# Causal attention in a four-layer block: score columns cut at 64 tokens, sums in a new order, and some masks moved to VectorE

## The chip, the cores and the metric

The kernel runs on one NeuronCore of a Trainium2 chip. The metric is the device time of one launch in microseconds (us), the median of a few runs. The engines are named TensorE (PE in the profile, its weight loads PEld), ScalarE (ACT), VectorE (DVE), GpSimd (POOL) and SyncE (SP, which here issues DMAs). Each engine works through its own instructions in order, and they wait for each other on semaphores.

## What is computed

The input is 16 sequences of 256 tokens of 128 numbers. Four layers follow each other, each added to the stream behind a layer norm: a long convolution, a mixture of eight experts, attention, and the experts again. The attention is where the change lies:

```python
qkv = x @ W_attn.T                       # 4 query sets, one k, one v; 16 heads of 8
for g in range(4):
    q = parts[g].reshape(B, T, 16, 8).transpose(0, 2, 1, 3)
    att = einsum('bhqd,bhkd->bhqk', q, k) * (1 / sqrt(8))
    att = softmax(where(causal, att, -inf))
    outs.append(einsum('bhqk,bhkd->bhqd', att, v))
out = concatenate(outs, -1) @ W_proj.T
```

So each head of each sequence has 4 x 256 queries against 256 keys, and a query sees only keys at or before its own place. In the kernel the second half of each sequence is stored backwards.

## The kernel before

The attention stage works on one sequence (a batch) at a time, and in it on four quads of four heads (lanes). The scores of a quad are made in four steps, so a batch has 16 steps and the stage 256. Scores stand with keys on the partitions and queries (four sets side by side) on the columns.

A step (`tensor_scores`) is three score matmuls of 512 columns, one from each of three lanes; a lane is 32 rows of TensorE. Into one half of a double buffer of three PSUM banks each (`TILE` = 1536 columns) go, by `STEPS_Q`, blocks of first keys (for which a lane needs 2 x 512 columns: four sets, both halves of the queries) and blocks of second keys (512 columns: four sets, the second half of the queries). ScalarE takes the exp of all 1536 columns at once (`scalar_exp`) into one of seven SBUF tiles (`prob`, `PROBS`). A score step may start when the exp two steps back has read its half of the buffer. GpSimd zeroes what lies beyond the diagonal with affine selects on blocks of 128 keys by 128 queries (`gpsimd_mask`, one or two instructions a step). Then TensorE sums v by these weights (`tensor_weigh`, four sums a quad: two of 512 columns, two of 256; the four lanes fill four 32-column parts of the array and add into bank 7). The sums have a column of ones in v, so the softmax denominator comes with them. They run one quad late: those of a quad are made in steps 1, 2 (two of them) and 3 of the next quad, the first of them after VectorE has read bank 7 (semaphore `turned`).

VectorE then transposes bank 7 (`vector_turn`), takes the reciprocal of the denominators and normalises. Beside that, by step number within a batch (`tensor_beside`, `vector_beside`), the other work of the batch is dealt out: step 0 transposes and splits the x of the batch after next (`tensor_at_x`, `vector_at_x_high`, `vector_at_x_low`), step 1 takes statistics for a norm, steps 4, 8 and 12 make and split q and k (`tensor_qk`, `vector_qk_high`, `vector_qk_low`), step 5 turns the output rows (`vector_rows`), steps 7 and 11 project them (`tensor_project`; VectorE adds them in `vector_attended` at its steps 6 and 10), steps 9 and 13 normalise two tiles, step 15 makes v of the next batch (`tensor_v`), which VectorE copies into place at its step 14 (`vector_v`). At steps 2 and 6 VectorE checks the denominators of an earlier batch against bounds (`vector_bounds`). q and k travel through DRAM into stacks of 32 rows a lane (`sync_stack`).

The order on TensorE in a step is: scores, what stands beside, then the sum. The order on VectorE:

```python
for n in range(LAST):
    if n % 4 == 3 and n >= 4:
        vector_turn(e, n // 4 - 1)
    vector_beside(e, *STARTS[n])
```

The functions that the change touches, and what calls them:

Of the kernel before, what the change touches and what calls it, by code (L numbers as in the profile page):

```python
# [17 lines left out]
P = 128  # L18
# [29 lines left out]
PAIRS = SETS // 2  # L48
# [4 lines left out]
BOTH = None  # L53
STEPS_Q = (((0, 0, 0), (1, 0, 0), (2, 1, BOTH)),
           ((2, 0, 0), (3, 0, 0), (0, 1, BOTH)),
           ((1, 1, BOTH), (3, 1, BOTH), (0, 0, 1)),
           ((1, 0, 1), (2, 0, 1), (3, 0, 1)))

SUMS_Q = ((0, 0, 1), (1, 0, 2), (1, 1, 2), (0, 1, 3))
STEPS_B = 4 * QUADS  # L60
PROBS = 7
# [74 lines left out]
def build_in(nc, dr, out, ctx):  # L136
# [28 lines left out]
    in_bounds = sb("in_bounds", [P, P])  # L165
# [47 lines left out]
    with ExitStack() as own:  # L213
# [5 lines left out]
        vstack = sb("vstack", [P, 2, HALVES, 2 * HD + HEADS * SLOT], of=own)  # L219
# [67 lines left out]
    def new_norm(tag):  # L287
# [42 lines left out]
    scored, exped, masked, weighed = (sem(n) for n in (  # L330
        "scored", "exped", "masked", "weighed"))
# [771 lines left out]
    def tensor_at_x(e, b):  # L1103
        e.wait_ge(mixed_norm.out, HALVES * b // FFN_TILES + 1)
        if b == 0:
            e.wait_ge(based, FFN_CHUNKS - 1)
        elif b == 2:

            e.wait_ge(accum, EXPERTS * FFN_CHUNKS - 1)
        else:  # L1110
            e.wait_ge(v_copied, max(1, b - 1))
        for h in range(HALVES):
            last = e.transpose(bank(at_bank(b))[:, h * P:(h + 1) * P], normed[:, HALVES * b + h, :], eye[:])
        last.then_inc(at_up, 1)


    def scalar_at_x_high(e, b):
        e.wait_ge(at_up, b + 1)
        e.copy(at_x[:, b % 2, 0, :], bank(at_bank(b))[:, 0:SEQ]).then_inc(at_high, 1)

    def vector_at_x_high(e, b):
        e.wait_ge(at_up, b + 1)
        e.wait_ge(v_up, b - 1)
        e.tensor_copy(at_x[:, b % 2, 0, :], bank(at_bank(b))[:, 0:SEQ]).then_inc(at_high, 1)

    def vector_at_x_low(e, b):
        e.wait_ge(at_high, b + 1)
        e.tensor_tensor(at_x[:, b % 2, 1, :], bank(at_bank(b))[:, 0:SEQ], at_x[:, b % 2, 0, :], ALU.subtract)\
# [79 lines left out]
    def tensor_v(e, b):  # L1208
# [7 lines left out]
        for h in range(HALVES):  # L1216
            for i, (w_part, x_part) in enumerate(PRODUCTS):
                last = e.matmul(bank(6)[:, h * P:(h + 1) * P], at_x[:, s, x_part, h * P:(h + 1) * P],
                                wqkv_parts[:, w_part, SETS + 1, :], start=(i == 0), stop=(i == len(PRODUCTS) - 1))
        last.then_inc(v_up, 1)  # L1220

    def v_places(b):
        return vstack[:, b % 2, :, 2 * HD:].rearrange("p h (n r) -> p h n r", r=SLOT)[:, :, :, 0:HD]

    def v_source():
        return bank(6)[:, 0:HALVES * D].rearrange("p (h n d) -> p h n d", n=HEADS, d=HD)

    def scalar_v_first(e):
        e.wait_ge(v_up, 1)
        e.wait_ge(zeroed, 3)  # L1230
        e.mul(v_places(0), v_source(), 1.0 / WSCALE).then_inc(v_copied, 1)

    def vector_v(e, b):
        e.wait_ge(v_up, b + 1)
        if b >= 2:
            e.wait_ge(weighed, STEPS_B * (b - 1))
        e.tensor_scalar(v_places(b), v_source(), 1.0 / WSCALE, None, ALU.mult).then_inc(v_copied, 1)
# [6 lines left out]
    def tensor_scores(e, n):  # L1244
# [12 lines left out]
        for i, (lane, keys, pair) in enumerate(STEPS_Q[t]):  # L1257
            at = slice(SLOT * lane, SLOT * (lane + 1))
            if keys == 0:
                queries = qstack[at, s, c, 2 * pair:2 * pair + 2, :].rearrange("p g (h q) -> p h g q", q=P)  # L1260
            else:
                queries = qstack[at, s, c, :, P:SEQ]
            last = e.matmul(to[:, i * BANK:(i + 1) * BANK], kstack[at, s, c, keys * P:(keys + 1) * P], queries, start=True,  # L1263
                            stop=True)
        last.then_inc(scored, 1)

    def scalar_exp(e, n):
        if n >= PROBS:
            q, t = divmod(n - PROBS, 4)
            e.wait_ge(weighed, 4 * q + (3 if t < 2 else 4))  # L1270
        e.wait_ge(scored, n + 1)
        e.activation(prob[:, n % PROBS, :], psum[:, TILE * (n % 2):TILE * (n % 2 + 1)], ACT.Exp, scale=SCALE)\  # L1272
# [4 lines left out]
    def gpsimd_masked(e, kept, second_keys):  # L1277
        sign = -1 if second_keys else 1
        return e.affine_select(kept, kept, [[0, kept.shape[1]], [0, 2], [sign, P]], ALU.is_ge, 0.0, base=0,  # L1279
                               channel_multiplier=-sign)  # L1280

    def gpsimd_mask(e, n):
        t = n % 4
        blocks = prob[:, n % PROBS, :].rearrange("p (n g q) -> p n g q", g=2, q=P)
        e.wait_ge(exped, n + 1)
        if t < 2:
            gpsimd_masked(e, blocks[:, 0:3:2], False)
            gpsimd_masked(e, blocks[:, 4:6], True).then_inc(masked, 1)
        elif t == 2:
            gpsimd_masked(e, blocks[:, 0:4], True)  # L1290
            gpsimd_masked(e, blocks[:, 4:5], False).then_inc(masked, 1)
        else:
            gpsimd_masked(e, blocks[:, 0:5:2], False).then_inc(masked, 1)

    def weights_of(n, lane, keys, pair):

        t, i = next((t, i) for t, banks in enumerate(STEPS_Q) for i, held in enumerate(banks)
                    if held[:2] == (lane, keys) and held[2] in (pair, BOTH))
        ring = prob[:, (n + t) % PROBS, i * BANK:(i + 1) * BANK]
# [885 lines left out]
```

## Time and profile before

| | |
|---|---|
| median of 3 runs | 800.98 us (800.91 to 801.03) |
| the profiled execution | 800.58 us |
| its span, first to last instruction | 798.9 us |
| attention stage (first scores to last exp) | 244.08 to 607.30 us of the span |
| PE / ACT / DVE / POOL busy | 95% / 90% / 81% / 70% of the span |
| mean granted TensorE clock | 0.996 |

Busy shares are means over stages with different limits. TensorE's rows are modelled at their ends: a row of matmuls is longer than the engine is held, so the distance between starts of what follows without a wait says more than a length.

### The profile page before, as it was taken

The numbers are of one execution on the slowest core, as the hardware profiler recorded it, in microseconds if no ns is written. First come the engines' busy times: TensorE is split into PE (matmuls) and PEld (weight loads), VectorE is DVE, ScalarE is ACT, GpSimd is POOL, SyncE is SP. The second block draws the span as 40 slices with busy tenths as digits, with TensorE's granted clock in tenths as the row PEclk, the third lists the DMA queues.
The fourth block names the chain that finished last, engine by engine and source line by source line (L and its number), as shares of the span: only waits on it lengthen the run. The fifth ranks groups of instructions, "written<-read, shape, count | busy, mean of one in ns | idle before, by whom it ended". The sixth has DMA issues, their size and how long they took to land.

```text
span 798.9 us, 20426 instructions
## 1 busy us (share of the span) xinstructions
PE 757.4 (95%) x7674; PEld 412.7 (52%) x7674; DVE 648.9 (81%) x1917; ACT 719.9 (90%) x932; POOL 560.2 (70%) x685
## 2 busy tenths in 40 slices
PE   5898999999999999999999999999999999999996
PEld 3345667777774333333333333333334777677774
DVE  7998999999876667777778787788566898989885
ACT  5918999999999999999999999999997999899984
POOL 2897676655437888888898888888896445444442
PEclk9999999999999999999999999999999999999999
DMA  9110000000133333442444334433500000000000
GB/s 279 61 70 29 1 2 2 2 2 1 23 94 99 98 90 89 90 99 78 96 108 106 90 88 92 90 78 96 106 2 2 1 15 16 15 14 16 15 15 18
DMA packets 37962, 45.70 MB, mean 57 GB/s; under 512 B 6137, under 2 KB 23810, under 8 KB 37858
## 3 DMA queue, kind: packets, MB, share of 16 engines
q1 hardware_dynamic: 37858, 44.33, 22.4%
q8 instruction: 63, 1.03, 0.6%
q14 instruction: 41, 0.34, 0.2%
HBM read 27.53 MB, written 16.78 MB: 55 GB/s over the span
## 4 chain that ended last, share of the span: by engine, by line
PE 56%; ACT 18%; DVE 12%; issue 10%; POOL 2%; DMA 0%; ACTq 0%; DVEq 0%; POOLq 0%
PE psum L1006 15%; PE psum L937 14%; ACT prob L1272 13%; PE psum L1316 12%; PE psum L1263 5%; PE psum L1374 4%; DVE mixed L1025 4%; PE psum L1154 2%; ACT hidden_first L951 2%; ACT hidden_parts_first L953 1%; PE psum L686 1%; DVE hidden_parts_first L960 1%; POOL yhat L666 1%; DVE prod L656 1%; DVE stats L362 1%
## 5 line engine op out<-in xcount | busy, mean ns | idle before, releaser
L1272 ACT ACTIVATE prob<-psum 128x1536 f32<-128x1536 f32 x256 | 347.6, 1503 | 14.5 <-PE psum L1263 14.5
L1279 POOL TENSOR_SCALAR_AFFINE_SELECT prob<-prob 128x512 f32<-128x512 f32 (+3 forms) x448 | 304.8, 709 | 42.2 <-ACT prob L1272 32.1
L1316 PE MATMUL psum<-prob,vstack 128*32 128x256 f32 (+1 forms) x2048 | 204.9, 495 | 1.6 <-DVE o_tok L1324 1.6
L937 PE MATMUL psum<-xt_parts,w_parts 128*128 128x512 f16 x768 | 186.6, 379 | 0.0
L1025 DVE SCALAR_TENSOR_TENSOR mixed<-psum,comb_y,mixed 128x128 f32<-128x128 f32 x512 | 143.1, 339 | 1.5 <-PE psum L1006 1.5
L967 POOL TENSOR_TENSOR hidden_parts_second<-hidden_second,hidden_parts_second 128x512 f16<-128x512 f32 x64 | 77.2, 1207 | 93.6 <-ACT hidden_parts_second L953 93.6
L967 POOL TENSOR_TENSOR hidden_parts_first<-hidden_first,hidden_parts_first 128x512 f16<-128x512 f32 x64 | 79.4, 1241 | 73.2 <-ACT hidden_parts_first L953 73.2
L1263 PE MATMUL psum<-qstack,kstack 32*128 32x512 f16 x768 | 99.8, 385 | 9.1 <-ACT prob L1272 7.7
L1263 PEld LDWEIGHTS psum<-qstack,kstack 32*128 32x128 f16 x768 | 24.9, 91 | 157.3 <-ACT prob L1272 138.7
L937 PEld LDWEIGHTS psum<-xt_parts,w_parts 128*128 128x128 f16 x768 | 71.0, 98 | 64.0 <-issue 1.4
L951 ACT ACTIVATE hidden_second<-psum,b 128x512 f32<-128x512 f32 x128 | 88.3, 690 | 15.6 <-PE psum L937 12.1
L1006 PEld LDWEIGHTS psum<-w_parts,hidden_parts_first 128*128 128x128 f16 x1536 | 90.4, 98 | 19.4 <-issue 6.1
L1006 PE MATMUL psum<-w_parts,hidden_parts_first 128*128 128x128 f16 x1536 | 96.2, 219 | 3.8 <-DVE mixed L1025 3.4
L1006 PEld LDWEIGHTS psum<-w_parts,hidden_parts_second 128*128 128x128 f16 x1536 | 90.9, 98 | 16.2 <-issue 2.1
L1006 PE MATMUL psum<-w_parts,hidden_parts_second 128*128 128x128 f16 x1536 | 96.0, 219 | 1.0 <-POOL hidden_parts_second L967 0.5
L951 ACT ACTIVATE hidden_first<-psum,b 128x512 f32<-128x512 f32 x128 | 90.4, 706 | 7.0 <-PE psum L937 6.2
L953 ACT ACTIVATE hidden_parts_first<-psum,b 128x512 f16<-128x512 f32 x128 | 90.6, 708 | 0.0
L953 ACT ACTIVATE hidden_parts_second<-psum,b 128x512 f16<-128x512 f32 x128 | 88.4, 691 | 0.0
L1324 DVE STREAM_TRANSPOSE o_tok<-psum 128x512 f32<-128x512 f32 x64 | 45.9, 716 | 44.5 <-PE psum L1316 43.6
L1316 PEld LDWEIGHTS psum<-prob,vstack 128*32 128x32 f32 x2048 | 46.8, 108 | 52.8 <-issue 29.4
L960 DVE TENSOR_TENSOR hidden_parts_second<-hidden_second,hidden_parts_second 128x512 f16<-128x512 f32 x64 | 56.2, 878 | 18.9 <-ACT hidden_parts_second L953 18.8
L960 DVE TENSOR_TENSOR hidden_parts_first<-hidden_first,hidden_parts_first 128x512 f16<-128x512 f32 x64 | 48.9, 765 | 14.9 <-ACT hidden_parts_first L953 14.9
(148 smaller groups left out, 840.9 us busy)
## 6 DMA issues: line engine op xcount, KB each, us to landing
qstack<-qk_parts SPq DMA_DIRECT2D x128, 128.0 KB, 3.6
qk_parts<-parts SPq DMA_DIRECT2D x64, 192.0 KB, 3.1
kstack<-qk_parts SPq DMA_DIRECT2D x128, 32.0 KB, 3.5
stream<-u_folded SPq DMA_DIRECT2D x4, 512.0 KB, 8.0
kept_x<-stream SPq DMA_DIRECT2D x4, 512.0 KB, 2.7
out<-mixed SPq DMA_DIRECT2D x7, 256.0 KB, 2.3
w_whole<-L_ffn_W SPq DMA_DIRECT2D x1, 1024.0 KB, 8.9
taps<-c_taps SPq DMA_DIRECT2D x1, 640.0 KB, 7.1
```

Of the source, the lines that this page charges most:

```text
L937: last = e.matmul(bank(u % 4), m.w1[:, w_part, ex, cols], xt_parts[:, s, x_part, :], start=(n == 0), stop=(n == len(PRODUCTS) - 1))
L951: last = e.activation(m.hidden[:, r, k, :], bank(u % 4), ACT.Relu, scale=scale, bias=bias)
L953: last = e.activation(m.hidden_parts[:, r, 0, k, :], bank(u % 4), ACT.Relu, scale=scale, bias=bias)
L960: e.tensor_tensor(m.hidden_parts[:, r, 1, 0, :], m.hidden[:, r, 0, :], m.hidden_parts[:, r, 0, 0, :], ALU.subtract).then_inc(low_first, 1)
L967: e.tensor_tensor(m.hidden_parts[:, r, 1, 1, :], m.hidden[:, r, 1, :], m.hidden_parts[:, r, 0, 1, :], ALU.subtract).then_inc(low_second, 1)
L1006: last = e.matmul(down_place(m, ch, ex, t), h_[:, t * P:(t + 1) * P], w_, start=(n == 0), stop=(n == len(terms) - 1))
L1025: last = e.scalar_tensor_tensor(out=m.y[:, t0 + t, :], in0=down_place(m, ch, ex, t), scalar=comb_y[:, s, t, ex:ex + 1], in1=m.y[:, t0 + t, ...
L1263: last = e.matmul(to[:, i * BANK:(i + 1) * BANK], kstack[at, s, c, keys * P:(keys + 1) * P], queries, start=True, stop=True)
L1272: e.activation(prob[:, n % PROBS, :], psum[:, TILE * (n % 2):TILE * (n % 2 + 1)], ACT.Exp, scale=SCALE)\
L1279: return e.affine_select(kept, kept, [[0, kept.shape[1]], [0, 2], [sign, P]], ALU.is_ge, 0.0, base=0, channel_multiplier=-sign)
L1316: last = e.matmul(to[SLOT * lane:SLOT * (lane + 1)], vstack[:, b % 2, keys, first:first + SLOT], weights_of(n - t, lane, keys, pair), star ...
L1324: e.transpose(o_tok[:, r, :], bank(7)).then_inc(turned, 1)
```

## The change

Everything is now cut at 64 tokens (`BLK`) instead of 128. Of the four blocks of 64 by 64 in each causal triangle one is never seen, and it is no longer computed. For a lane there are three kinds of scores: EARLY (the first 64 keys of each half against all queries of that half, 512 columns), LATE (the other 64 keys of each half against the later 64 queries, 256 columns), and ACROSS (keys of the second half against queries of the first, in stored order, 512 columns, all seen in full, without a mask). A step holds two banks of EARLY or ACROSS and 256 columns of LATE: 1280 columns (`COLS`). Keys of both halves lie on partitions 0 to 63 and 64 to 127, so each block of scores takes two matmuls of 64 output rows, six a step. The sums are three a quad, ACROSS first, then EARLY, then LATE (256 columns), one each in steps 1, 2 and 3 of the next quad. v lies in three arrangements, which takes more and smaller products (`tensor_v`) and three copies (`v_moves`); `tensor_at_x` transposes the second half twice; `vector_rows` takes three transposes; the bounds are checked every four batches on four times the width. The ring has eight exp tiles.

GpSimd masks 768 columns (the EARLY banks and the LATE part) of steps 0 and 1 twice each, one pass for each half, and the LATE parts of steps 2 and 3 together (512 columns) twice, in quads 0 and 2 of a batch. In quads 1 and 3 VectorE masks those 512 columns by one multiply with a table `seen` of zeros and ones, built once.

```diff
-SUMS_Q = ((0, 0, 1), (1, 0, 2), (1, 1, 2), (0, 1, 3))
+STEPS_Q = (((EARLY, 0, 0), (EARLY, 1, BANK), (LATE, 2, 2 * BANK)),
+           ((EARLY, 2, 0), (EARLY, 3, BANK), (LATE, 1, 2 * BANK)),
+           ((ACROSS, 0, 0), (ACROSS, 1, BANK), (LATE, 3, 2 * BANK)),
+           ((ACROSS, 2, 0), (ACROSS, 3, BANK), (LATE, 0, 2 * BANK)))
+COLS = 2 * BANK + SETS * BLK
+SUMS_Q = (ACROSS, EARLY, LATE)
+VECTOR_LATE = (1, 3)
+PROBS = 8
+BOUNDED = 4
 tensor_at_x:
-        for h in range(HALVES):
+        for at, h in ((0, 1), (P, 1), (P + BLK, 0)):
 tensor_v:
-        for h in range(HALVES):
+        for kind in (EARLY, LATE, ACROSS):
             for i, (w_part, x_part) in enumerate(PRODUCTS):
+                for half in range(HALVES if kind != ACROSS else 1):
+                    rows = slice(BLK * half, BLK * (half + 1)) if kind != ACROSS else slice(0, P)
+    def v_moves(b):
+        for half in range(HALVES):
+            rows = slice(BLK * half, BLK * (half + 1))
+            yield places[rows, 0:2, :, half], source[rows, 0:2]
+        yield places[:, ACROSS, :, 0], source[:, ACROSS]
 tensor_scores:
+            for half in range(HALVES):
+                rows = slice(BLK * half, BLK * (half + 1))
+                if kind == EARLY:
+                    key, moving, place = P * half, queries[:, half], to[rows, col:col + BANK]
+                elif kind == LATE:
+                    key, moving, place = P * half + BLK, queries[:, half, 1], to[rows, col:col + SETS * BLK]
+                else:
+                    key, moving, place = P + BLK * half, queries[:, 0], to[rows, col:col + BANK]
+                last = e.matmul(place, kstack[at, s, c, key:key + BLK], moving, start=True, stop=True)
+    def vector_late(e, q):
+        e.wait_ge(exped, 4 * (q + 1))
+        if q == VECTOR_LATE[0]:
+            e.wait_ge(seen_set, 3)
+        kept = late_place(q)
+        e.tensor_tensor(kept, kept, seen[:].rearrange("p (n g q) -> p n g q", n=1, g=1).to_broadcast([P, 2, SETS, BLK]),
+                        ALU.mult).then_inc(late_multiplied, 1)
+    def gpsimd_mask(e, n):
+        q, t = divmod(n, 4)
+        if t == 0:
+            gpsimd_early_second_half(e, q, 0)
+            if q and (q - 1) % QUADS not in VECTOR_LATE:
+                gpsimd_late_first_half(e, q - 1)
+        elif t == 1:
+            gpsimd_early_second_half(e, q, 1)
+            gpsimd_early_first_half(e, q, 0)
+            gpsimd_early_first_half(e, q, 1)
+        elif t == 3 and q % QUADS not in VECTOR_LATE:
+            gpsimd_late_second_half(e, q)
 tensor_weigh, before a LATE sum:
+            e.wait_ge(late_multiplied if c in VECTOR_LATE else late_masked, late_count(q))
 vector_rows:
-        e.transpose(o_rows[:].rearrange("p a h k t -> p (a h k t)"), o_norm[:].rearrange("p a n r -> p (a n r)"))\
+        for late in range(2):
+            e.transpose(rows[:, :, 1 - late], blocks[:, :, late])
+        e.transpose(o_rows[:, 1].rearrange("p g t -> p (g t)"), o_norm[:, 1].rearrange("p n r -> p (n r)"))\
 vector_attention:
             vector_beside(e, *STARTS[n])
+            if n % 4 == 1 and n >= 4 and (n // 4 - 1) % QUADS in VECTOR_LATE:
+                vector_late(e, n // 4 - 1)
```

## Rows read from the trace of the kernel before

**Rows 1.** Stages: batches 0, 7, 14, 15; columns: stretch, length, busy us (instructions).

```profile
core 0: us, PE busy (x) PEld busy (x) DVE busy (x) ACT busy (x) POOL busy (x), PEclk, DMA share, GB/s
244.08:266.16 22.08, 20.27 (x218) 8.19 (x217) 15.04 (x41) 21.38 (x17) 19.46 (x28) 1.00 0.30 75
402.06:424.70 22.64, 22.34 (x219) 8.18 (x215) 17.36 (x39) 21.71 (x17) 20.07 (x30) 1.00 0.44 95
...
561.14:583.33 22.19, 20.23 (x202) 6.75 (x198) 10.65 (x22) 21.64 (x17) 19.10 (x29) 1.00 0.42 87
583.33:607.30 23.97, 20.92 (x212) 7.26 (x212) 18.17 (x59) 23.53 (x20) 22.30 (x32) 1.00 0.01 2
```

**Rows 2.** ScalarE: timeline (start, length, instructions) and a group (busy, mean ns).

```profile
397.40 16.23 ACT L1272 ACTIVATE prob<-psum 128x1536 f32<-128x1536 f32 x12 [0.66 <-PE psum L1263]
413.90 1.45 ACT L1272 ACTIVATE prob<-psum 128x1536 f32<-128x1536 f32 x1 [0.28 <-PE psum L1263]
L951 ACT ACTIVATE hidden_second<-psum,b 128x512 f32<-128x512 f32 x128 | 88.3, 690 | 15.6 <-PE psum L937 12.1
```

**Rows 3.** TensorE: timeline of one inner batch.

```profile
400.63 0.51 PE L1218 MATMUL psum<-wqkv_parts,at_x 128*128 128x128 f16 x6
401.06 1.07 PE L1316 MATMUL psum<-prob,vstack 128*32 128x512 f32 x8
402.06 0.39 PE L1263 MATMUL psum<-qstack,kstack 32*128 32x512 f16 x3
402.39 0.44 PE L1113 MATMUL psum<-eye,normed 128*128 128x128 f32 x2
402.93 0.39 PE L1263 MATMUL psum<-qstack,kstack 32*128 32x512 f16 x3
403.25 1.07 PE L1316 MATMUL psum<-prob,vstack 128*32 128x512 f32 x8
...
404.60 1.07 PE L1316 MATMUL psum<-prob,vstack 128*32 128x256 f32 x16
...
405.94 1.07 PE L1316 MATMUL psum<-prob,vstack 128*32 128x512 f32 x8
406.96 0.39 PE L1263 MATMUL psum<-qstack,kstack 32*128 32x512 f16 x3
407.29 0.83 PE L1154 MATMUL psum<-at_x,wqkv_parts 128*128 128x256 f16 x6
...
411.32 1.16 PE L1374 MATMUL psum<-wproj,o_rows 128*128 128x128 f32 x8
...
413.40 0.39 PE L1263 MATMUL psum<-qstack,kstack 32*128 32x512 f16 x3
...
419.54 0.39 PE L1263 MATMUL psum<-qstack,kstack 32*128 32x512 f16 x3
```

**Rows 4.** Waits in 402.06 to 424.70: us in total, times, longest.

```profile
PEld psum L1263 <- ACT prob L1272: 8.4, 13, 0.9
```

**Rows 5.** VectorE: timeline in the same batch.

```profile
401.17 0.42 DVE L1237 TENSOR_SCALAR vstack<-psum 128x256 f32<-128x256 f32 x1 [0.70 <-PE psum L1218]
402.20 0.72 DVE L1324 STREAM_TRANSPOSE o_tok<-psum 128x512 f32<-128x512 f32 x1 [0.60 <-PE psum L1316]
...
403.34 0.82 DVE L1329 TENSOR_TENSOR o_norm<-o_tok,rden 128x256 f32<-128x256 f32 x1
...
406.25 0.74 DVE L1352 SCALAR_TENSOR_TENSOR in_bounds<-rden,in_bounds 128x128 f32<-128x128 f32 x1
407.07 0.72 DVE L1324 STREAM_TRANSPOSE o_tok<-psum 128x512 f32<-128x512 f32 x1
...
408.21 0.49 DVE L1329 TENSOR_TENSOR o_norm<-o_tok,rden 128x256 f32<-128x256 f32 x1
...
409.34 0.69 DVE L1184 SCALAR_TENSOR_TENSOR parts<-psum,parts 128x512 f16<-128x512 f32 x1
409.95 1.23 DVE L1339 STREAM_TRANSPOSE o_rows<-o_norm 128x1024 f32<-128x1024 f32 x1
```

**Rows 6.** GpSimd: mask groups by shape, 300 to 590 us (busy, mean ns).

```profile
L1279 POOL TENSOR_SCALAR_AFFINE_SELECT prob<-prob 128x512 f32<-128x512 f32 x204 | 126.1, 643 | 31.2 <-ACT prob L1272 26.6
L1279 POOL TENSOR_SCALAR_AFFINE_SELECT prob<-prob 128x768 f32<-128x768 f32 x51 | 44.5, 872 | 0.0
```

**Rows 7.** GpSimd and VectorE at 586.79: a bounds instruction behind the end of two masks.

```profile
585.61 1.23 POOL L1279 TENSOR_SCALAR_AFFINE_SELECT prob<-prob 128x512 f32<-128x512 f32 x2 [0.40 <-ACT prob L1272]
586.79 0.28 DVE L1352 SCALAR_TENSOR_TENSOR in_bounds<-rden,in_bounds 128x128 f32<-128x128 f32 x1
```

**Rows 8.** VectorE: the normalising group in 402.07 to 424.70 (busy, mean ns).

```profile
L382 DVE TENSOR_SCALAR normed<-stream,meanvar,rstd 128x128 f32<-128x128 f32 x4 | 1.5, 428 | 0.0
```

**Rows 9.** GpSimd: the clearing in the first expert stage.

```profile
137.95 1.86 POOL L1637 MEMSET vstack<- 128x2112 f32 x1
```

More of the change, by code:

```diff
@@ L1256, in tensor_scores @@
             e.wait_ge(s_stack[s], STACK * (b // 2 + 1))
-        for i, (lane, keys, pair) in enumerate(STEPS_Q[t]):
+        for kind, lane, col in STEPS_Q[t]:
             at = slice(SLOT * lane, SLOT * (lane + 1))
[L1259 to L1264, printed above, removed]
+            queries = qstack[at, s, c].rearrange("p g (h l q) -> p h l g q", h=HALVES, q=BLK)
+            for half in range(HALVES):
[7 more added lines that the diff above has]
+                last = e.matmul(place, kstack[at, s, c, key:key + BLK], moving, start=True, stop=True)
         last.then_inc(scored, 1)
@@ L1295, in weights_of, with gpsimd_masked @@
[L1295 to L1299, printed above, removed]
-        return ring if keys == 0 else ring[:, pair * SEQ:(pair + 1) * SEQ]
-    def tensor_weigh(e, n):
-        b, c, t = step_of(n)
-        keys, pair, needs = SUMS_Q[t]
-        if n % STEPS_B == 0:
-            e.wait_ge(v_copied, b + 1)
-        if n == 0:
-            e.wait_ge(accum, EXPERTS * FFN_CHUNKS)
-        elif t == 0:
-            e.wait_ge(turned, n // 4)
-        e.wait_ge(masked, n - t + needs + 1)
-        to = bank(7) if keys == 0 else bank(7)[:, SEQ:2 * SEQ]
+    def gpsimd_masked(e, kept, half):
+        sign = 1 if half else -1
+        return e.affine_select(kept, kept, [[0, n] for n in kept.shape[1:-1]] + [[sign, BLK]], ALU.is_ge, 0.0,
+                               base=BLK * half, channel_multiplier=-sign)
@@ new lines, in gpsimd_mask, with weights_of @@
+    def gpsimd_mask(e, n):
+        q, t = divmod(n, 4)
[9 more added lines that the diff above has]
+            gpsimd_late_second_half(e, q)
+    def weights_of(q, kind, lane):
+        t, col = next((t, at) for t, held in enumerate(STEPS_Q) for of, head, at in held if (of, head) == (kind, lane))
+        return prob[:, (4 * q + t) % PROBS, col:col + (SETS * BLK if kind == LATE else BANK)]
@@ L1314, in tensor_weigh @@
         for lane in range(LANES):
[L1315 to L1317 removed]
+            last = e.matmul(to[SLOT * lane:SLOT * (lane + 1)],
+                            vstack[:, b % 2, kind, c * LANES + lane].rearrange("p h r -> p (h r)"),
+                            weights_of(q, kind, lane), start=(kind == ACROSS), stop=(kind == LATE))
```

180 lines of the change are left out of this document (102 added, 78 removed).

## The prediction

> **What bounds the kernel now.** I read four views: the stages, the waits, one batch of the attention stage instruction by instruction on three engines, and the groups by shape.
>
> The change touches the attention stage, 244.08 to 607.30 us of the span. Its 16 batches take about 22.64 us each, the first 22.08 and the last two 22.19 and 23.97 [rows 1]. In an inner batch ScalarE is busy 21.7 us, TensorE 22.3, VectorE 17.4 and GpSimd 20.1, so no engine has much room. ScalarE's exp of 1536 columns is the pace: twelve in a row fill 16.23 us, that is one alone (1.45) and eleven at 1.344 [rows 2]. Sixteen make 21.5; the missing 1.1 us comes at the two projections, where TensorE is late.
>
> TensorE is hardly slower than that pace. From starts that follow each other [rows 3]: three score matmuls S = 0.33 (402.93 to 403.25), a weighted sum over 512 columns W = 1.00 (405.94 to 406.96 is 1.02), two sums of 256 columns together also 1.0, so one alone about 0.57 (half the 0.86 of streaming, and the 0.14 that any sum has beside it), V = 0.44, transposes A = 0.45, q and k products Q = 0.76 (0.83 less the drain that overlaps) twice and 0.43 for the half-sized third, projection P = 1.09. A batch: 16 S + 12 W + 5.0 (V, A, 2 Q and the third, 2 P) = 22.3 of 22.64. That the score loads wait 8.4 us for ScalarE [rows 4] is mostly loads standing ready early: matmuls behind them still run. So if ScalarE gets faster, TensorE follows at once, and then it matters who else is late.
>
> VectorE is [rows 5]. After the v copy (401.17) and the turn of a quad (402.20) it works without a gap until 407.0, and the next turn (407.07) starts just when its sum is ready (405.94 + 1.02). The rows of the projection end at 411.18 and the projection starts at 411.32. Both times it is just in time.
>
> **The change part by part.** I name quads of a batch c0 to c3 and steps n0 to n15; the three sums of a quad run in the steps 1, 2 and 3 of the next quad (c3's in n1 to n3 of the next batch).
>
> *ScalarE.* 256 columns less an exp. From 512 columns (690 ns) to 1536 (1.45 us alone) the slope is 0.74 ns a column; the mean of the pace is 0.875 [rows 2]. I take 0.21 us: pace 1.13, 18.1 a batch. That alone would be 256 x 0.21 = 54 us, if nothing else bound.
>
> *TensorE.* Sums: across 512, early 512, late 256: 2.57 for 3.0 a quad, 1.7 less a batch. Scores: the same 32-row lanes, each as two halves of 64 output rows, six matmuls for three. That column parts of the array run beside each other the sums show (8 matmuls on four 32-column parts in 1.07 us), that row parts do the scores (three in 0.39) [rows 3]; both at once no row shows. Bounds: 0.33 if they overlap, 0.33 + 0.21 if a lane's halves run after each other. The rows show both kinds of overlap, so I take 0.33. V becomes 15 matmuls, 12 of them half wide: between 9 and 15 pitches of 0.055 and a switch (V's 0.44 is six such and 0.11), 0.6 to 1.05 for 0.44; I take 0.75. The transposes A: three for two, 0.60. Sum of a batch: 16 x 0.33 + 4 x 2.57 + (0.60 + 1.95 + 0.75 + 2.18) = 21.0. So TensorE alone would already stop the pace far above ScalarE's 18.1.
>
> *GpSimd.* Four masks of 768 columns a quad (mean 872, pitch 0.82) and, in every second quad, two of 512 (pitch 0.59) [rows 6]: 15.5 a batch for about 19. It has room, but its instructions are longer.
>
> *VectorE.* Added: the late multiply of 512 columns twice a batch. No row has it; the nearest is 0.68 to 0.69 (512 columns, 409.34) [rows 5]. The v copy is three instructions: 0.42 + 0.42 + 0.29 and gaps, 0.97 to 1.3, for 0.42. The rows' transpose is three for one of 1.23: between 0 and 0.4 more, I take 0.25. The bounds go from two a batch (0.74 the one at 406.25) to two, four times as wide, in four batches.
>
> *What a multiply waits for.* An instruction of VectorE with two SBUF tensors stands while GpSimd is in a mask: the bounds of 128 columns took 0.74 at 406.25, with masks running, and 0.28 at 586.79, where the mask had just ended [rows 5, 7]. The normalisation of a quad took 0.82 and 0.49 likewise. A running mask of 768 can therefore cost the multiply 0 to 0.86; I take 0.35. (The Trainium skill, "SBUF — State Buffer", on who interferes with whom: the port pair is held by whichever starts first for its whole instruction, and the other is blocked. The trace agrees, 0.74 against 0.28; without the rule the multiply would be 0.69 flat and the forecast about 6 us lower, 0.35 in 12 first stretches and some 0.1 in 12 fourth ones.)
>
> *The new wait.* The late sum of c3 (step n3) now waits for the multiply, which stands in VectorE's order behind the v copy, the turn of c2, its reciprocal and normalisation, the two x copies and the statistics of step n1. Count from the end of V. VectorE: v starts at 0.11 and ends at 1.31; the turn to where the bounds instruction now starts is 402.20 to 406.25, 4.05, less 0.2 for a mean normalisation: 5.2; lock 0.35, multiply 0.69, signal 0.13 (as from the rows' end 411.18 to 411.32), and 0.1 of gaps: 6.47. TensorE is ready after late c2 0.57, S, A 0.60, and S + W twice, S: 4.5. So it stands about 2 us, with everything behind the sum on its in-order queue: next scores, hence ScalarE.
>
> Against the batch before, stretch by stretch [rows 3, 5]:
> - scores n0 to the end of c3's last sum: 4.90 before (402.06 to 406.96). Now 6.47 + 0.57 less the 0.57 of late c2 at the head = 6.47. **+1.57**
> - from there to the projection: 4.36 before (to 411.32). VectorE now 0.11 + 4.11 (407.07 to 411.18) + 0.25 + 0.13 = 4.60; TensorE alone 4.08. **+0.24**
> - projection and last sum: 2.08 before (to 413.40), now 1.09 + 0.57. **-0.42**
> - n8 to the end of c1's last sum: 6.14 before (413.40 to 419.54). Now VectorE: 0.11, turn, reciprocal, normalisation and q/k copies 2.96 (407.07 to 410.03), two tiles normalised 0.43 + 0.43 [rows 8], lock, multiply and signal 1.17, in all 5.1, against TensorE's 5.2 (4 S, Q, 2 W, P); then 0.57: 5.8. **-0.35**
> - n12 to n0: 5.16 before (to 424.70), now 4 S + 0.43 + 2 W + 0.75 + 0.57 = 5.07. **-0.09**
>
> Sum +0.95 for an inner batch. Of these there are 11 (2 to 11 and 13): +10.5. Batch 12, whose range checks already slow it, +0.6. Batch 1 has no statistics in n1 (1.5 less in the chain): -0.5. Batch 0 has neither chain nor projection: near ScalarE's pace, 19.5 for 22.08: -2.6. Batch 14 has no q and k work: about 20.3 for 22.19, -1.9. Batch 15 likewise, with its waits for v: 21.1 for 23.97, -2.9. GpSimd's clearing of v places grows from 2112 to 3072 columns (1.86 us, so 0.9 more [rows 9]) and the table's selects; in the expert stage GpSimd idles over a microsecond an expert, I charge 0.5. Together +3.7. The expert stages are as before. The profiled execution took 800.58 (span 798.9 and 1.7 around it), 0.4 under the median of 800.98; so 804.7 for the median.
>
> **The rivals.**
> 1. *The chain on VectorE is short* (multiply not blocked, normalisation 0.42, v 0.97, rows no longer): the first stretch +0.79, then 0, -0.42, -0.49, -0.25 = -0.37 a batch; with the edge batches' -7.4 that is 12 x -0.37 - 7.4 = -11.8, so 789, and up to 799 where only some of these hold. For it: the phases of masks and VectorE shift, and 0.42 occurs. Against: GpSimd still masks 15.5 of 23 us, three masks in a row just at step n1. It decides where the multiply is done within 5.5 us of V's end.
> 2. *TensorE alone bounds*: 21.0 a batch, 12 x -1.6 and the edges -8: about 773. It needs VectorE's chain under 4.5 us, and even the shortest count gives 5.7.
> 3. *ScalarE goes on setting the pace*: 801 - 54 = 747. TensorE's sum speaks against it.
> 4. *A lane's halves do not overlap*: +0.21 a step. Where VectorE sets the stretch it hides, elsewhere it shows. By stretch: 6.47 unchanged, 4.9 and 6.0 plus 0.57 where TensorE now leads, 5.9 for 5.07, so about 2 us a batch on my case and some 3 in each edge batch: 804.7 + 12 x 2 + 4 x 3 = 841. For it: no row has both partings at once. (The Trainium skill, "TensorEngine Tiling (Array Packing)", tiling modes, lists 32x64 as eight independent tiles, and under restrictions that column tiling gives up the fast weight load; the trace has no score load of 64 columns, and the first would keep 0.33, the second puts it towards this rival.)
>
> **How the numbers follow.** My case 0.55, and as it reaches from 799 to 822 with the bounds of lock and v, I put 0.15 of it within 0.2% (1.6 us, about what a measurement of this kernel can tell from no change) and 0.40 above. Rival 1 0.22, rival 2 0.10, rival 3 0.03, rival 4 0.10. So faster 0.35, same 0.15, slower 0.50. The range runs from rival 1's low end, 789, to my case with its unknown terms at their upper ends: the lock 0.86 for 0.35 at both multiplies, the normalisation at its full 0.82, the rows 0.4 longer for 0.25, 1.4 a batch in 12 batches, 17 us, so 822. With 0.77 for these two cases and a little of the others that fall inside, it holds about 0.8.
>
> **What would show it.** Exps at a pace of 1.13 where they follow each other; an inner batch of 23.6 us; score groups still 0.33 to the next start; in step n3 a TensorE wait of about 2 us for the multiply, the largest new row of the waits; multiplies of 0.69 and of over 1 us; GpSimd down to some 70% of a batch. If the wait in n3 is under 1 us or score groups take 0.5, the prediction is wrong there.

## The result and the profile after

The changed kernel takes 823.46 us (822.05 to 825.52, four executions) against 800.94 for the kernel before: ratio 1.0285, interval 1.026 to 1.031. It is slower by 22.5 us, and outside my range, which ended at 822. In the profiled executions (the one after was the longest of its four) the span went from 798.9 to 823.8, so 24.9 us more: 1.5 ahead of the attention stage (first scores at 245.59 instead of 244.08), 23.0 in it, 0.4 behind it.

The windows of an inner batch and, below it, of a stretch in batch 0 that is taken up again under the clock; they answer to [rows 1] and have its columns:

```profile
core 0: us, PE busy (x) PEld busy (x) DVE busy (x) ACT busy (x) POOL busy (x), PEclk, DMA share, GB/s
389.49:413.78 24.29, 21.25 (x245) 7.77 (x242) 20.58 (x44) 19.32 (x17) 18.64 (x23) 1.00 0.40 88
264.00:268.30 4.30, 4.30 (x35) 0.71 (x34) 3.38 (x7) 3.32 (x3) 3.28 (x5) 0.60 0.20 43
```

An inner batch takes 24.29 us (22.64 before). ScalarE is down to 19.3 of it and GpSimd to 18.6, as meant; VectorE is up from 17.4 to 20.6. What TensorE waits for is in the waits of the stretch 365.70 to 389.50, in which L1348 is the multiply, L1387 the sums, L1296 the scores, L1417 the rows and L1454 the projection (this batch is one of the two with the wide bounds instruction, 0.42 us longer than the others):

```profile
ACT prob L1303 <- PE psum L1296: 4.8, 4, 1.7
PEld psum L1387 <- DVE prob L1348: 2.6, 2, 1.5
PE psum L1387 <- DVE prob L1348: 2.1, 2, 1.2
...
PEld psum L1454 <- DVE o_rows L1417: 1.2, 1, 1.2
PE psum L1454 <- DVE o_rows L1417: 0.9, 1, 0.9
```

The late sums stand twice a batch for the multiply, 2.1 us, and ScalarE stands for the scores behind them. The places are in TensorE's timeline:

```profile
365.63 0.52 PE L1127 MATMUL psum<-eye,normed 128*128 128x128 f32 x3 [0.44 <-DVE vstack L1264]
...
367.75 1.07 PE L1387 MATMUL psum<-prob,vstack 128*32 128x512 f32 x8
368.75 0.41 PE L1296 MATMUL psum<-qstack,kstack 32*64 32x512 f16 x6
370.35 0.64 PE L1387 MATMUL psum<-prob,vstack 128*32 128x256 f32 x8 [1.19 <-DVE prob L1348]
...
381.77 1.16 PE L1454 MATMUL psum<-wproj,o_rows 128*128 128x128 f32 x8
383.85 0.64 PE L1387 MATMUL psum<-prob,vstack 128*32 128x256 f32 x8 [0.92 <-DVE prob L1348]
...
388.19 0.80 PE L1238 MATMUL psum<-wqkv_parts,at_x 128*64 128x128 f16 x15
388.92 0.64 PE L1387 MATMUL psum<-prob,vstack 128*32 128x256 f32 x8
389.49 0.41 PE L1296 MATMUL psum<-qstack,kstack 32*64 32x512 f16 x6
```

The first wait for the multiply (step n3, quad c3) I had forecast, the second (step n11, quad c1) not, nor the 0.44 us that the transposes A (L1127) wait for the three v copies. VectorE's timeline shows what stood in front of each multiply:

```profile
366.87 0.41 DVE L1141 CAST at_x<-psum 128x256 f16<-128x256 f32 x1
367.32 0.42 DVE L1145 TENSOR_TENSOR at_x<-psum,at_x 128x256 f16<-128x256 f32 x1
367.66 0.86 DVE L374 BATCH_NORM_STATS2 stats<-stream 128x6 f32<-128x128 f32 x4
368.56 0.38 DVE L378 BATCH_NORM_AGGREGATE meanvar<-stats 128x2 f32<-128x6 f32 x4
368.97 0.74 DVE L384 TENSOR_SCALAR vareps<-meanvar 128x4 f32<-128x4 f32 x1
369.61 0.68 DVE L1348 TENSOR_TENSOR prob<-prob,seen 128x512 f32<-128x512 f32 x1
...
380.00 0.69 DVE L1201 SCALAR_TENSOR_TENSOR parts<-psum,parts 128x512 f16<-128x512 f32 x1
380.60 1.87 DVE L394 TENSOR_SCALAR normed<-stream,meanvar,rstd 128x128 f32<-128x128 f32 x2
382.39 1.40 DVE L1348 TENSOR_TENSOR prob<-prob,seen 128x512 f32<-128x512 f32 x1
```

GpSimd's timeline beside them:

```profile
367.92 3.14 POOL L1312 TENSOR_SCALAR_AFFINE_SELECT prob<-prob 128x768 f32<-128x768 f32 x3 [0.20 <-ACT prob L1303]
...
380.63 3.68 POOL L1312 TENSOR_SCALAR_AFFINE_SELECT prob<-prob 128x768 f32<-128x768 f32 x4 [0.22 <-ACT prob L1303]
```

In the first place an instruction over four columns (L384) takes 0.74 us, and the multiply behind it 0.68. In the second the two normalisings take 1.87 together, where one alone had a mean of 0.43 [rows 8], and the multiply takes 1.40. Both lie inside a run of masks. I call such an instruction held: its row is longer than that of the same instruction elsewhere. It goes both ways: the last of the three masks from 367.92 begins at 369.64, just behind the start of the free multiply, and lasts 1.42 us where the two before it last 0.91.

I cut each batch by the starts of scores n0, n4, of the projection, of n8, n12 and the next n0, as in the prediction:

| inner batch | n0-n4 | -projection | -n8 | n8-n12 | n12-n0 | sum |
|---|---|---|---|---|---|---|
| before | 4.90 | 4.36 | 2.08 | 6.14 | 5.16 | 22.64 |
| forecast | 6.47 | 4.60 | 1.66 | 5.79 | 5.07 | 23.6 |
| measured | 6.13 | 4.66 | 1.66 | 6.75 | 5.08 | 24.29 |

(24.71 in the two inner batches with the wide bounds instruction, 1.38 us.) Batch 0 takes 24.25, batch 13 27.4, batches 14 and 15 20.42 and 25.34.

### The profile page after: what moved, and what is told of

Same layout as the page of the kernel before. It is cut to its first block, busy times and chain, and to the rows that moved or that the text cites. A ratio compares the mean times of both kernels' runs of the same rounds, so it can differ in the third digit from the quotient of the medians.

```text
span 823.8 us, 21206 instructions
## 1 busy us (share of the span) xinstructions
PE 746.6 (91%) x8090; PEld 407.9 (50%) x8090; DVE 702.7 (85%) x1987; ACT 681.1 (83%) x934; POOL 539.0 (65%) x562
## 4 chain that ended last, share of the span: by engine, by line
PE 49%; DVE 35%; issue 7%; ACT 5%; POOL 3%; DMA 0%; DVEq 0%; ACTq 0%; POOLq 0%
PE psum L1018 14%; PE psum L949 13%; PE psum L1387 10%; DVE mixed L1037 4%; DVE o_tok L1397 4%; DVE normed L394 3%; DVE prob L1348 3%; PE psum L1454 2%; PE psum L1296 2%; DVE parts L1196 2%; DVE vstack L1264 2%; DVE stats L374 2%; DVE rden L1400 2%; ACT hidden_parts_first L965 2%; ACT hidden_first L963 2%
## 5 line engine op out<-in xcount | busy, mean ns | idle before, releaser
L1303 ACT ACTIVATE prob<-psum 128x1280 f32<-128x1280 f32 x256 | 307.8, 1238 | 76.1 <-PE psum L1296 68.3
L1312 POOL TENSOR_SCALAR_AFFINE_SELECT prob<-prob 128x768 f32<-128x768 f32 (+1 forms) x320 | 282.7, 913 | 85.5 <-ACT prob L1303 84.5
L1387 PE MATMUL psum<-prob,vstack 128*32 128x512 f32 (+1 forms) x1536 | 181.5, 545 | 33.0 <-DVE prob L1348 28.4
L1296 PE MATMUL psum<-qstack,kstack 32*64 32x512 f16 (+1 forms) x1536 | 104.5, 366 | 1.2 <-ACT prob L1303 1.1
L1296 PEld LDWEIGHTS psum<-qstack,kstack 32*64 32x64 f16 x1536 | 30.0, 101 | 149.2 <-ACT prob L1303 117.6
L1387 PEld LDWEIGHTS psum<-prob,vstack 128*32 128x32 f32 x1536 | 30.5, 109 | 74.6 <-DVE prob L1348 35.7
```

The costliest lines, as they stand in the source:

```text
L1296: last = e.matmul(place, kstack[at, s, c, key:key + BLK], moving, start=True, stop=True)
L1303: e.activation(prob[:, n % PROBS, 0:COLS], psum[:, TILE * (n % 2):TILE * (n % 2) + COLS], ACT.Exp, scale=SCALE)\
L1312: return e.affine_select(kept, kept, [[0, n] for n in kept.shape[1:-1]] + [[sign, BLK]], ALU.is_ge, 0.0, base=BLK * half, channel_multipli ...
L1387: last = e.matmul(to[SLOT * lane:SLOT * (lane + 1)], vstack[:, b % 2, kind, c * LANES + lane].rearrange("p h r -> p (h r)"), weights_of(q, ...
```

## The experiments

All edits are on the changed kernel unless said otherwise; ratios are to the kernel before, whose medians lay near 800.9. Stretches are cut as above, in batch 2.

### All masks on GpSimd

```diff
-VECTOR_LATE = (1, 3)
+VECTOR_LATE = ()
 VectorE, in the second expert stage:
-                    vector_late(e, LAST // 4 - 1)
 gpsimd_attention, at its end:
+        gpsimd_late_first_half(e, LAST // 4 - 1)
```

> The changed kernel with GpSimd masking the late keys of every quad, as it does in quads 0 and 2; no multiply on VectorE. In the changed kernel an inner batch takes 24.29 us, in stretches 6.13 (scores n0 to n4), 4.66 (to the projection), 1.66, 6.75 (n8 to n12) and 5.08. Theory A, the late sums of quads 3 and 1 wait for the multiply behind VectorE's other work: the first stretch falls to about 4.9 and the fourth to 5.8, as in batch 1 of the changed kernel (4.87, 5.76), the others stay; a batch of 22.1, the clock no longer falls, and the whole is 788 to 795 us. Theory B, GpSimd is too full (19 us of masks and rstd in a batch of 22, and its masks hold up VectorE's two-input instructions): late sums wait for GpSimd instead, batches of 23 us or more, 805 us or more. Theory C, the loss is in TensorE's smaller products and the v copies: batches stay over 23.5 us and the whole over 815.

Measured: 791.58 us (791.37 to 791.95), ratio 0.9872 [0.9843, 0.9901]; stretches 4.87, 4.35, 1.66, 5.76, 5.08, in all 21.72. Theory A holds: without the multiplies on VectorE the change is no longer slow. With GpSimd doing all the masks the rest of the change gains 0.92 us a batch on the kernel before, and in an inner batch TensorE never waits for GpSimd (in the whole stage twice, 1.7 us together). This version beats both kernels, by 1.3% the one before. The clock did not behave as expected: it still falls once, just behind the stage. An inner batch is 0.7 us above the 21.0 that I had counted for TensorE alone; its two waits for VectorE, 0.44 and 0.18, are most of that:

```profile
PE psum L1127 <- DVE vstack L1264: 0.4, 1, 0.4
PE psum L1454 <- DVE o_rows L1417: 0.2, 1, 0.2
```

### The multiply on 8 of 512 columns

The late keys of quads 1 and 3 stay nearly unmasked here.

```diff
-        kept = late_place(q)
-        e.tensor_tensor(kept, kept, seen[:].rearrange(...).to_broadcast([P, 2, SETS, BLK]),
+        kept = late_place(q)[:, :, :, 0:1]
+        e.tensor_tensor(kept, kept, seen[:, 0:1].rearrange(...).to_broadcast([P, 2, SETS, 1]),
```

> The changed kernel with the multiply cut to one column of each block of 64 (8 columns of 512), in the same place of VectorE's order; the late keys of quads 1 and 3 are left unmasked but for these. Theory A in the form 'its place in the order costs': only the instruction's own 0.5 to 0.6 us goes each time, stretches 5.6 and 6.2, batch 23.2, whole about 805. In the form 'the instruction itself, with its wait for masks, costs': also the blocked time of the second one (1.40 against 0.68) goes, stretches 5.6 and 5.8 or less, batch 22.8, whole about 798. Theory C: 818 or more.

Measured: 809.8 us (808.25 to 811.06), ratio 1.0096 [1.0063, 1.013]; 5.62, 4.67, 1.66, 6.24, 5.08, in all 23.25. Its VectorE timeline:

```profile
293.81 0.74 DVE L384 TENSOR_SCALAR vareps<-meanvar 128x4 f32<-128x4 f32 x1
294.45 0.16 DVE L1348 TENSOR_TENSOR prob<-prob,seen 128x8 f32<-128x8 f32 x1
```

The arithmetic of the multiplies, 0.52 each, is worth 1.04 of the 2.57 us a batch (24.29 less the 21.72 with none); the place in VectorE's order and what is held there are worth the rest. That is the first form of the expectation; the whole is 5 us above it, and part of that is a clock fall in batch 13. In batches 2 to 11 the small multiplies take 0.16 or 0.88 (five of the 32, outside these batches, 0.50 to 0.87): the 0.72 of being held is the same for 8 columns as for 512.

### The multiply ahead of the work beside

```diff
+            if n % 4 == 0 and n >= 4 and (n // 4 - 1) % QUADS in VECTOR_LATE:
+                vector_late(e, n // 4 - 1)
             vector_beside(e, *STARTS[n])
-            if n % 4 == 1 and n >= 4 and (n // 4 - 1) % QUADS in VECTOR_LATE:
-                vector_late(e, n // 4 - 1)
```

> The changed kernel with the multiply at the head of VectorE's work of the step before (step 0 and 8 instead of the end of step 1 and 9), so ahead of the x copies and statistics, and ahead of the q and k copies and the norm. Theory A: nothing waits for it any more, stretches one and four fall to 4.9 and 5.8, but the work behind it is later by 0.7 to 1.4 us: q and k of step 8 and the projections may wait; batch 22.1 to 22.6, whole 788 to 800. Theory B, the multiply is blocked by masks wherever it stands and delays the rest of VectorE as much: the waits move to the projection and to bank 6, batch 23.5 or more, whole over 812. Theory C: over 818.

Measured: 805.25 us (803.0 to 806.51), ratio 1.0045 [1.003, 1.006]; 4.87, 5.21, 1.66, 5.76, 5.08, in all 22.59. The waits of the late sums are gone, so both stalls are a matter of the queue. But the work did not vanish. Against the first experiment's kernel the stretch to the projection is 5.21 instead of 4.35, since the rows (L1417) now come late (TensorE waits 0.66 us for them); c3's multiply is itself held, 1.38 us, where it now stands. Of the 2.57 us a batch a third is given back there, more in the two batches with the wide bounds (23.5), and the whole came out 5 us above theory A's range.

### The clearing split

```diff
-        e.memset(vstack[:], 0.0).then_inc(zeroed, 1)
+    def gpsimd_clear_first(e, s):
+        e.memset(vstack[:, s], 0.0).then_inc(zeroed, 1)
...
+                if (ch, ex) in ((3, 1), (3, 3)):
+                    gpsimd_clear_first(e, ex // 2)
```

with the table built two experts later.

> The changed kernel with GpSimd's clearing of the v places, ones, bounds and table spread over four experts of the first expert stage instead of one. In the changed kernel the first scores start 1.5 us later than before (245.59 against 244.08) and the hidden blocks fall behind between 142 and 155 us. If the longer clearing is the cause, the first scores come at 244 to 244.3 and the whole is 1.3 us shorter (0.15%, hardly more than the spread); if it is not, they stay at 245.6.

Measured: 821.92 us (821.63 to 825.28), ratio 1.0263 [1.0225, 1.0301]. First scores at 245.21, of 245.59: between my two outcomes. The hidden blocks near 150 us are 0.5 behind the kernel before instead of 1.4, but the expert stage loses another 0.7 at 222 us, in this kernel and the changed one alike. The inner batches are unchanged at 24.28. Its profile serves for the clock, below.

### The q and k copies on ScalarE

```diff
-            vector_qk_high(e, b + 2, at // 4 - 1)
 scalar_attention, behind scalar_exp(e, n):
+            if b + 2 < BATCH and at in (4, 8, 12):
+                if at == 4:
+                    e.wait_ge(s_parts[b % 2], 64 * ((b + 2) // 2))
+                scalar_qk_high(e, b + 2, at // 4 - 1)
```

> The changed kernel with the three copies of q and k of steps 4, 8 and 12 (0.68 us each on VectorE) given to ScalarE, which idles 5 us of a batch there. Stretches of the changed kernel: 6.13, 4.66, 1.66, 6.75, 5.08. Theory A, a chain in VectorE's order: the first stretch has no such copy in its chain and stays 6.13, the second falls by up to 0.6 to TensorE's own 4.1, the fourth by about 0.7 to 6.0 or 6.1, or by more where the multiply then falls between masks; batch 22.9 to 23.1, whole 800 to 808. Rival, VectorE is simply too full (its share of busy time counts, not what stands ahead of the sum): every stretch shortens, the first too. Rival, ScalarE's exps come late behind the copies: no gain, 820 or more.

Measured: 804.88 us (803.68 to 806.07), ratio 1.0044 [1.0031, 1.0057]; 6.13, 4.31, 1.66, 5.76, 5.08, in all 22.95, as expected. With 0.68 us less in front of it the multiply of c1 is also free, at 0.68, so the whole 0.99 of the fourth stretch goes. The first, where no copy was moved, keeps its 6.13.

### Masks of one column in 64

GpSimd leaves nearly all masking out, VectorE's multiply is whole.

```diff
+        few = 1 if len(kept.shape) > 3 else BLK
+        if few == 1:
+            kept = kept[:, :, :, 0:1]
-        return e.affine_select(kept, kept, [...] + [[sign, BLK]],
+        return e.affine_select(kept, kept, [...] + [[sign, few]],
```

> The changed kernel with GpSimd's masks cut to one column in 64, so that GpSimd hardly reads SBUF beside VectorE; nearly all masking of quads' early keys and of quads 0 and 2 is left out, the table and VectorE's multiplies stay whole. Theory B, masks hold up VectorE's instructions: all multiplies take 0.68 instead of 0.68 and 1.40, the normalising of two tiles ahead of the second takes 0.7 us instead of 1.9; stretch four falls from 6.75 to 5.76, TensorE's own; stretch one has no held-up multiply and stays within 0.1 of 6.13; batch 23.2, whole about 805. If the masks don't hold VectorE up, nothing changes: 24.3 and 823.

Measured: 792.48 us (792.18 to 793.1), ratio 0.9893 [0.9874, 0.9912]; 5.58, 4.36, 1.66, 5.76, 5.08, in all 22.43. VectorE's groups in 291.9 to 316.2 (busy, mean ns), first of the changed kernel:

```profile
L394 DVE TENSOR_SCALAR normed<-mixed,meanvar,rstd 128x128 f32<-128x128 f32 x4 | 3.2, 850 | 0.0
L1348 DVE TENSOR_TENSOR prob<-prob,seen 128x512 f32<-128x512 f32 x2 | 2.1, 1040 | 0.0
L384 DVE TENSOR_SCALAR vareps<-meanvar 128x4 f32<-128x4 f32 x1 | 0.7, 740 | 0.0
```

and of this kernel, where L1351 is the multiply:

```profile
L1351 DVE TENSOR_TENSOR prob<-prob,seen 128x512 f32<-128x512 f32 x3 | 2.1, 685 | 0.0
L394 DVE TENSOR_SCALAR normed<-mixed,meanvar,rstd 128x128 f32<-128x128 f32 x4 | 1.2, 373 | 0.0
L384 DVE TENSOR_SCALAR vareps<-meanvar 128x4 f32<-128x4 f32 x1 | 0.2, 170 | 0.0
```

Same instructions, same shapes; only GpSimd's masks are short. All 32 multiplies take 0.68 to 0.69 here. So the masks hold them, not only the multiply but also the norm's instructions, which read and write one tensor each in SBUF (and read per-partition scalars beside it). Being held is worth 24.29 - 22.43 = 1.86 us a batch. The whole kernel is 31 us faster, but that is not all holding: this kernel has no clock fall either, and the falls of the changed kernel took about 6 us of its profiled execution (below). I had expected only the fourth stretch to fall; the first fell too, by 0.55, the length by which L384 had been held.

### The exp back to 1536 columns, all masks on GpSimd

On the first experiment's kernel; the 256 columns more are values that nothing reads.

```diff
-prob[:, n % PROBS, 0:COLS], psum[:, TILE * (n % 2):TILE * (n % 2) + COLS]
+prob[:, n % PROBS, 0:TILE], psum[:, TILE * (n % 2):TILE * (n % 2) + TILE]
```

> The kernel with all late keys masked by GpSimd (791.6 us, batch 21.72), but each exp over 1536 columns as before the change; the last 256 columns are left over values that nothing reads. It tells what the narrower exp is worth. By my count of TensorE (21.0 to 21.7 a batch with ScalarE at 18.1) the fewer columns are worth only what lies between TensorE's 21.7 and ScalarE's old pace with its stalls, 22.6: batch 22.5 to 22.7, edges 1 us each, whole 803 to 807. Rival, the whole gain comes from TensorE's smaller sums and the exp is worth nothing: 792 to 794. Rival, ScalarE set the pace all along: 0.21 x 256, 840 or more.

Measured: 796.11 us (793.43 to 797.84), ratio 0.9934 [0.9912, 0.9956]; 5.02, 4.37, 1.66, 5.76, 5.08, in all 21.89. My count missed, the rival came near: the shorter exp is worth 0.17 us an inner batch of the 0.92. The medians differ by 4.5 us, but of that the clock has a part: in the profiled execution it is at half for 6.9 us in batch 15, which takes 26.27 instead of 22.52. The rest of the inner batch's gain is TensorE's, above all the third and fourth stretches (1.66 for 2.08, 5.76 for 6.14) with their smaller sums.

### All masks on GpSimd, copies on ScalarE, clearing split

The edits of the first, fourth and fifth experiments together.

> Late keys of all quads on GpSimd, q and k copies on ScalarE, the clearing spread over four experts. From 791.6 us: the second stretch 4.35 falls to TensorE's own 4.1 (-3 us in 12 batches, and some in batches 12 and 13), the first scores come 0.4 to 1.4 us earlier; 785 to 788. Rival, ScalarE (18.1 and 1.5 us of a batch of 21.5) now comes late with its exps at the copies: 792 or more.

Measured: 791.55 us (790.82 to 792.25), ratio 0.9881 [0.9861, 0.9901]; 4.87, 4.53, 1.66, 5.76, 5.08, in all 21.90. The rival's mechanism was right, at the edge of its 792: the copy now queues behind an exp on ScalarE, VectorE waits 0.82 us for it and the rows come later, so TensorE waits 0.35 us for them instead of 0.18. There was little to win on VectorE by then.

### One multiply at a time

```diff
-VECTOR_LATE = (1, 3)
+VECTOR_LATE = (3,)
```

> The changed kernel with VectorE masking the late keys of quad 3 alone, GpSimd those of quad 1 too. If the two waits add up stretch by stretch: 6.13 for the first stretch as with both, 5.76 for the fourth as with none, batch 23.3, whole 806 to 810. If they interact (GpSimd's fuller row of masks shifts what VectorE is held up by), the first stretch moves by more than 0.3 from 6.13.

Measured: 808.31 us (807.31 to 810.0), ratio 1.0093 [1.0059, 1.0126]; 6.13, 4.67, 1.66, 5.76, 5.08, in all 23.30. And with `VECTOR_LATE = (1,)`:

> The changed kernel with VectorE masking the late keys of quad 1 alone. Added stretch by stretch: 4.87 for the first as with none, 6.75 for the fourth as with both, batch 22.7 to 23.0, whole 801 to 807. If the fourth stretch falls to 6.1 or less, its extra time came from how the masks fell and not from the multiply's place.

Measured: 806.56 us (804.37 to 808.85), ratio 1.0066 [1.0045, 1.0086]; 4.87, 4.35, 1.66, 6.76, 5.08, in all 22.72. Both as expected (the second has a clock fall in batch 0, the first none), and they add up: c3's multiply costs 1.58 a batch (first and second stretch), c1's 1.00 (fourth), together the 2.57 between 21.72 and 24.29.

### The turn ahead of the v copy

On the first and fourth experiments' edits: the turn of c2 before the v copy, the transposes A in step 3, the x copies in step 2.

```diff
-        if b + 2 < BATCH and at == 0:
-            tensor_at_x(e, b + 2)
+        if b + 2 < BATCH and at == 3:
+            tensor_at_x(e, b + 2)
 and in vector_beside: vector_at_x_high at 2 (of 0), vector_v at 15 (of 14)
```

> All late keys on GpSimd, the clearing spread, and the step before the batch's end reordered: VectorE turns quad 2 before it copies v, TensorE's transposes of x come in step 3 instead of step 0 and VectorE's x copies in step 2. In the kernel with all late keys on GpSimd the transposes of step 0 wait 0.4 us for the three v copies to leave bank 6. If that wait is what the first stretch of 4.87 holds over TensorE's own 4.4, it falls to 4.4 to 4.7, batch 21.3 to 21.5, whole 785 to 790. Rival: the x copies now come late for q and k of step 4, the second stretch grows by as much, whole 791 or more.

Measured: 796.06 us (794.43 to 796.52), ratio 0.9931 [0.9907, 0.9955]; 4.62, 4.55, 1.66, 5.76, 5.08, in all 21.67. The rival was right: the first stretch gave 0.25, as expected, and the second took 0.20 back. Batch 15 lost 2.9 us (25.37 for 22.52): in its step n0 TensorE waits 2.67 us for the v copies, and the clock falls to half for 3.5 us behind it. As a whole this order is worse than the plain one.

## Why the prediction was wrong

The sign was right, and so was the mechanism of the first stretch, a late sum that waits for VectorE's chain and multiply. The size was not: I forecast 3.7 us more, the spans differ by 24.9.

**What held.** Score groups of six matmuls are 0.34 to the next start (366.08 to 366.42), so rival 4 is out: halves of a lane overlap. V takes 0.73 (388.19 to 388.92) for my 0.75. The third stretch is 1.66 and the fifth 5.08, both as counted. The second is 4.66 for 4.60. Batch 1 is 0.6 faster, batch 14 1.8, as forecast (0.5 and 1.9). The wait in step n3 is there, 1.19 us for the 2 I gave. The multiply of c3 was not held (0.68, I had 1.04), but L384 in front of it was (0.74, alone 0.17), and from V's end to the late sum it was 6.14 us (364.21 to 370.35) for my 6.47. TensorE was ready 0.44 later than I counted, because its transposes A wait for the v copies; that shortens the wait, not the stretch, which came out 0.34 shorter than I said. I had put 0.35 of holding on the multiply, and 0.57 fell on L384 instead: that this stretch came out near is partly luck. Rivals 1 to 3 needed a short chain on VectorE; taking the multiply off VectorE altogether gives 791.6, near rival 1's low end, and even then it isn't rival 2's 773. (Rival 1's fourth stretch, 0.49 less, lay below what I had counted for TensorE alone, 5.2 + 0.57; with the multiplies gone it is 0.38 less.)

**The step that failed** is the fourth stretch, "-0.35": it came out +0.61, 0.96 worse in each of ten batches, and batches 0 and 13 have the same 6.75. I had VectorE done with the multiply of c1 after 5.1 us, just ahead of TensorE's 5.2. The late sum started after 6.19 (377.66 to 383.85), so VectorE's chain ended last, by a microsecond. Two terms of it were too small. I charged "two tiles normalised 0.43 + 0.43" from a mean of the kernel before [rows 8]; the pair took 1.79 from its start to the multiply's. And I gave a lock of 0.35; the multiply took 1.40, so 0.72 of holding. I had applied the rule of being held to the instructions with two SBUF tensors alone. The masks-cut kernel shows that the norm's instructions are held too (0.373 for 0.850 us on average), and the mean of rows 8 already hid one: of its four instructions three last 0.34 to 0.38 and one 0.66, the same in every batch from 300 to 425 us. And I had spread the hold as a mean, while each of batches 2 to 11 repeats the last to 0.01 us: there the multiply of c3 is always free and that of c1 always held. What the hold comes to depends on the place: besides 0.72, L384 has 0.57 here, 0.07 in the inner batches of the first experiment's kernel (0.24 us), and four multiplies in batches 12, 14 and 15 have 0.34 to 0.55. I think that a late multiply moves the next exps and their masks with it, so that the same instruction meets the same mask in each batch; no run tests that.

**The edge batches.** Of the miss of 21 us the ten batches 2 to 11 have 7.8, for in them the first stretch pays back a third. Batches 0, 13 and 15 have 12.8 (24.25, 27.4, 25.34 against my 19.5, 23.6, 21.1), the start of the stage 1.0 and the end 0.4; batch 12 is 0.8 better than I said (23.02 for 23.8). For batch 0 I had counted no chain on VectorE, but c1's multiply stands there too: TensorE waits 2.01 us for it. With all masks on GpSimd these three batches take 20.75, 22.50 and 22.52, together 1.6 over my counts, so nearly all of the 12.8 comes with the multiplies. Part of that is the same holding: with the masks cut they take 20.0, 23.1 and 21.3. Part is TensorE's clock. In the profile after, the granted clock is at half (the 1.2 GHz level) at 264.3 to 267.8, 564.7 to 571.5 and 626.2 to 629.6 us; before, it stays whole through the attention stage. At half, eight sums last 1.94 us where they last 1.06:

```profile
262.61 0.64 PE L1387 MATMUL psum<-prob,vstack 128*32 128x256 f32 x8 [2.01 <-DVE prob L1348]
...
263.95 0.41 PE L1296 MATMUL psum<-qstack,kstack 32*64 32x512 f16 x6
264.29 1.94 PE L1387 MATMUL psum<-prob,vstack 128*32 128x512 f32 x8
266.16 0.64 PE L1296 MATMUL psum<-qstack,kstack 32*64 32x512 f16 x6
266.73 1.54 PE L1387 MATMUL psum<-prob,vstack 128*32 128x512 f32 x8
```

The kernel with the split clearing has the same inner batches and no fall inside the stage; its batches 0, 13 and 15 take 22.67, 24.77 and 23.44. The differences, 1.6, 2.6 and 1.9, put the cost of the falls in the profiled execution at 6.1 us, some of which that kernel loses again to a fall just behind the stage (its rest is 2.9 longer). The median is 2 us below the profiled execution, so it may hold less of them.

**The start.** I charged 0.5 for the clearing and the table, and the stage starts 1.5 later. GpSimd's group in the first expert stage lasts 4.55 us instead of 2.2, and the hidden block behind it starts 1.4 later; the idle time there did not cover it, though half a microsecond comes back by 162 us. But the clearing is not all of it, since spreading it gave back only 0.4. At 222 us the changed kernel and the split-clearing one both lose 0.7 (0.3 of it comes back): there ScalarE waits for the fifteen products V of batch 0, 0.5 us with the split clearing, and copies them in three instructions instead of one. I had charged nothing for that.

**What stays open.** Why the clock falls where it does isn't settled: ahead of 264.3 and of 564.7 the split-clearing kernel has the same TensorE stalls of 2 us and does not fall there. That masks hold the norm's instructions is shown by cutting the masks; that they do so through a shared way into SBUF is only argued. (The Trainium skill, "SBUF — State Buffer", on who interferes with whom, puts it down to a shared port pair, and names beside instructions with two SBUF inputs those of VectorE in a two-port mode, which I had passed over. The runs agree in that either engine is held by the other, and in that the holds of the attention stage given here, 0.07 to 0.72, are all shorter than a mask; whether the norm's instructions run in that mode no run shows.) Nor have I traced why batch 13 is slower than the other inner batches even with the masks cut (23.09 for 22.43).

## What to carry to other kernels

Before moving work from an idle-looking engine to another, list what stands in front of it in the new queue, at its held duration: the masks had room on GpSimd (with all of them there the kernel takes 791.6 us, and no other version is clearly faster), and the multiplies cost 2.57 us a batch on VectorE for 1.4 us of work. Where two engines can hold each other, count each instruction at the place that the schedule gives it, as free or as held, up to the length of the other's instruction, and do the forecast for both; where the batches repeat each other, the same case comes in all of them. And put edge batches into the sum with the same care as inner ones: here three of sixteen carried 12.8 of the 21 us.

## What was unexpected of the hardware

- A VectorE instruction on four columns, one SBUF tensor in and out, lasts 0.17 us free and 0.74 beside a mask (0.24 at another place); one of 128 columns has a mean of 0.37 with short masks and 0.85 with long ones.
- A group of six 32-row matmuls into 64 output rows, four of 512 columns and two of 256, is 0.34 us to the next start, the same as three of 512 columns into 128 rows (0.33): a lane's two halves run side by side.
- 256 columns less an exp bring the pace of exps in a row to 1.12 to 1.13 from 1.344 us, and are worth 0.17 us a batch of 16 when TensorE sets the pace.
- The holding goes both ways: a mask of 0.91 us takes 1.42 where a VectorE multiply started just ahead of it.
- The granted clock fell to half (1.2 GHz) for 3.4 to 6.9 us at three places of the attention stage of the changed kernel, and at one place each with c1's multiply alone (264.2 us), the 8-column multiply (552.6), the copies on ScalarE (547.4), the full exp (583.4) and the turn first (575.4). Each time TensorE had just waited: once for 1.4 to 2.7 us, with the full exp three times for 0.4 to 0.9. The other kernels, with the one before and the one with all masks on GpSimd, have no fall in that stage. The stall doesn't bring it every time: the split-clearing kernel has the two of 2 us, without a fall.
